# Second context attention: the first batch's keys projected in the norm's stage, and two sets of banks for the first unit's scan

## The reference, cut to what matters

```
q = (layernorm(x) @ Wq + bq)   k = (context @ Wk + bk)   v = (context @ Wv + bv)   (per head)
attn = clip(q k^T * 8**-0.5, -10000, 10000)
attn = softmax(attn)           (where any is nan: 1/1601)
x = x + (attn v) @ Wo + bo
```

## Time and profile before

| | |
|---|---|
| median of 3 runs | 4416.74 us (4416.56 to 4418.13) |
| profiled execution: span from the first to the last instruction | 4419.3 us, 2.6 above the median; no other time is recorded for it |
| busy: PE, DVE, ACT, POOL | 3412.6, 2996.2, 1886.4, 352.4 us |
| mean granted TensorE clock | 0.872 |
| this attention's stages, preparing stage to the end of the ticks | 1788.3 to about 2407 us |

### The profile page before, as it was taken

The page is one execution under the profiler, slowest core; times in us unless marked ns, Lnnn a source line. Parts: engine busy times, 40 slices in busy tenths (PEclk is TensorE's granted clock), DMA queues, the critical chain, the costliest instruction groups (busy, mean ns, idle before and its releaser), DMA issues. The chain is left out here.

```text
span 4419.3 us, 53028 instructions
## 1 busy us (share of the span) xinstructions
PE 3412.6 (77%) x21138; PEld 1815.2 (41%) x21138; DVE 2996.2 (68%) x4093; ACT 1886.4 (43%) x2165; POOL 352.4 (8%) x150
## 2 busy tenths in 40 slices
PE   5799999999999975577776786266654669577579
PEld 3434444444444433234333654222222346454357
DVE  4467776777677767388998545689998554546642
ACT  2255555555555543134443133344443134345233
POOL 0000000000000000100000000024443000000000
PEclk9799999999999987699999798566666798688789
DMA  2000000000000000100000300100000101010000
GB/s 79 9 0 0 0 1 0 0 0 0 0 1 0 0 6 7 25 14 9 9 1 3 117 2 2 46 0 0 0 0 0 39 2 39 9 39 1 1 31 14
DMA packets 13082, 56.19 MB, mean 13 GB/s; under 512 B 2209, under 2 KB 2721, under 8 KB 12066
## 3 DMA queue, kind: packets, MB, share of 16 engines
q1 hardware_dynamic: 12834, 52.78, 3.9%
HBM read 48.97 MB, written 0.52 MB: 11 GB/s over the span
## 5 line engine op out<-in xcount | busy, mean ns | idle before, releaser
L1019 PE MATMUL banks<-L0x_q_context,L0x_context 96*128 96x512 f32 x1600 | 725.7, 596 | 11.2 <-ACT L0x_ring L1086 9.9
L1030 PE MATMUL banks<-L0x_ring,L0x_context_rows 128*101 128x512 f32 x1600 | 721.3, 594 | 2.9 <-ACT L0x_ring L1076 2.9
L1086 ACT COPY L0x_ring<-banks 128x1024 f32<-128x1024 f32 (+1 forms) x416 | 404.3, 980 | 604.5 <-PE banks L1019 604.5
L1130 DVE TENSOR_TENSOR L0x_maxima<-L0x_maxima,L0x_ring 128x1024 f32<-128x1024 f32 (+1 forms) x288 | 332.7, 1165 | 228.3 <-ACT L0x_ring L1086 228.2
L1114 DVE TENSOR_TENSOR L0x_ring<-L0x_ring,L0x_greatest 128x2048 f32<-128x2048 f32 (+1 forms) x208 | 466.5, 2245 | 20.8 <-ACT L0x_ring L1086 19.3
L1019 PEld LDWEIGHTS banks<-L0x_q_context,L0x_context 96*128 96x128 f32 x1600 | 303.0, 191 | 396.9 <-issue 375.9
L1030 PEld LDWEIGHTS banks<-L0x_ring,L0x_context_rows 128*101 128x101 f32 x1600 | 267.8, 168 | 411.6 <-issue 406.4
L1076 ACT ACTIVATE L0x_ring<-L0x_ring 128x2048 f32<-128x2048 f32 (+1 forms) x208 | 384.2, 1848 | 11.1 <-DVE L0x_ring L1114 10.7
L1521 ACT ACTIVATE L1x_probs<-banks 128x2048 f32<-128x2048 f32 (+1 forms) x112 | 196.6, 1755 | 260.3 <-PE banks L1451 218.4
L1554 DVE TENSOR_REDUCE L1x_maxima<-banks 128x3 f32<-128x1203 f32 (+1 forms) x176 | 241.6, 1373 | 92.3 <-PE banks L1420 92.3
L1420 PE MATMUL banks<-L1x_k,L1x_q 32*128 32x401 f32 x1024 | 181.4, 591 | 120.4 <-DVE L1x_maxima L1554 105.1
(11 more groups left out here) (943 smaller groups left out, 5258.2 us busy)
## 6 DMA issues: line engine op xcount, KB each, us to landing
L1f_expert_weights<-in_L1f_experts SPq DMA_DIRECT2D x16, 512.0 KB, 10.3
L2f_expert_weights<-in_L2f_experts SPq DMA_DIRECT2D x8, 512.0 KB, 5.3
L3a_expert_weights<-in_L3a_experts SPq DMA_DIRECT2D x8, 512.0 KB, 6.0
L3f_expert_weights<-in_L3f_experts SPq DMA_DIRECT2D x8, 512.0 KB, 6.5
L1x_k<-L1x_k_rows SPq DMA_DIRECT2D x64, 50.0 KB
L0x_context<-in_context SPq DMA_DIRECT2D x1, 2401.5 KB, 19.6
L1x_context<-in_context SPq DMA_DIRECT2D x4, 600.4 KB, 5.2
L2x_contexts<-in_context SPq DMA_DIRECT2D x1, 2401.5 KB, 18.2
```

The costliest lines, as they stand in the source:

```text
L1019: mm = pe.matmul(k.ps[0:height(j), i, :], c1[:, j * P:j * P + height(j)], q1[:, u // 2 % 2, :], start=True, stop=True)
L1030: mm = pe.matmul(k.ps[0:CW, bank, :], rows1[0:height(j), j, :], ring[0:height(j), s % RING, i, :], start=s == FIRST[u] and i == 0, stop=s ...
L1086: act.copy(ring[0:r, s % RING, 2 * p:2 * p + len(pair), :], k.ps[0:r, 2 * p:2 * p + len(pair), :]).then_inc(copied, 1)
L1130: dve.tensor_tensor(o, before, ring[0:r, s % RING, 2 * p:2 * p + m, :], ALU.max).then_inc(maxed, 1)
```

## The change

For the first batch the key projection, its bias and the spreading DMAs leave `attend_clipped` and go to the stage of the norm, as an object `FirstKeys` that `normalise_columns` calls: first in PE's list, after the root in ACT's, alone in SP's. The first unit's scan uses banks 0 to 2 for even bursts and 3 to 5 for odd ones, and waits for the reduce of the burst before last. The slot of the first batch's values comes after the first unit's turn, and the first three slots alternate with the first three of the second unit's bursts.

```diff
@@ normalise_columns(..., keys=None)
+        if keys:
+            @block.sync
+            def _(sp):
+                keys.spread(sp)
         @block.tensor
         def _(pe):
+            if keys:
+                keys.project(pe)
             for t in range(tiles):
@@
             act.activation(k.sd[:, 0:tiles], k.ve[:, 0:tiles], ACT.Sqrt).then_inc(sd_ready, 1)
+            if keys:
+                keys.place(act)
@@
-X_SLOTS = [("keys", 0), ("values", 0), ("floor", 0), ("pair", 0)]
+X_SLOTS = [("values", 0), ("floor", 0), ("pair", 0)]
@@
+class FirstKeys:
+    def project(self, pe):
+        pe.wait_ge(self.arrived[0], 16)
+        for i, (c, m) in enumerate(CHUNKS):
+            mm = pe.matmul(self.k.ps[:, 3 + i, 0:m], self.w["k"], self.context[:, 0, c:c + m], start=True, stop=True)
+        mm.then_inc(self.projected, 1)
+    def place(self, act):
+        act.wait_ge(self.projected, 1)
+        act.activation(self.k_rows[:], self.k.ps[:, 3:7, :].rearrange("p a n -> p (a n)")[:, 0:CTX], ACT.Identity,
+                       bias=self.w["bk"]).then_inc(self.placed, 1)
+    def spread(self, sp):
+        d = 8
+        sp.wait_ge(self.placed, 1)
+        for h in range(16):
+            sp.dma_start(self.kT[32 * (h % 4):32 * (h % 4) + d, 0, h // 4, :], self.k_rows[d * h:d * h + d, :]).then_inc(self.here, 16)
@@ attend_clipped
+        def scan_bank(m):
+            return 3 if m < NB and m % 2 else 0
@@ SP
-            spread(0)
             load(2)
@@ scan(m)
-                if g == 0 and burst == 0:
-                    pe.wait_ge(spread_keys, 16 * H * (b + 1))
+                if u == 0 and burst == 0:
+                    pe.wait_ge(first_keys.here, 16 * H)
+                elif g == 0 and burst == 0:
+                    pe.wait_ge(spread_keys, 16 * H * b)
-                if m:
+                if u == 0 and m >= 2:
+                    pe.wait_ge(reduced, m - 1)
+                elif u:
                     pe.wait_ge(reduced, m)
@@ PE, ahead of the loop
-            for slot in X_SLOTS[0:2]:
-                fill(slot)
             for m in range(NB):
                 scan(m)
             turn(0)
-            for slot in X_SLOTS[2:FIRST_SLOTS]:
+            early = [m for n in range(SCAN_FROM, 0) for m in bursts_in(n)]
+            for i, slot in enumerate(X_SLOTS[0:FIRST_SLOTS]):
                 fill(slot)
-            for n in range(SCAN_FROM, 0):
-                for m in bursts_in(n):
-                    scan(m)
+                scan(early[i])
+            for m in early[FIRST_SLOTS:]:
+                scan(m)
```

More of the change, by code:

```diff
@@ L223, with normalise_columns @@
 ACT_TILES = (3, 6, 7)
-def normalise_columns(k, src, rows, dstT, gain=None, shift=None, column_gain=None, column_shift=None, eps=1e-5, values=None, tiles=TILES):
+def normalise_columns(k, src, rows, dstT, gain=None, shift=None, column_gain=None, column_shift=None, eps=1e-5, values=None, tiles=TILES, keys=None):
     shared = [t for t in ACT_TILES if t < tiles] if gain is None else ()
@@ L1365, with __init__, attend_clipped @@
 SLOT = {slot: n for n, slot in enumerate(X_SLOTS)}
-def attend_clipped(k, w, qT, context, c_sum, marks, limit, pick, y, arrived, bufs):
+class FirstKeys:
+    def __init__(self, k, ctx, w, context, arrived, k_rows, kT):
+        self.k, self.w, self.context, self.arrived, self.k_rows, self.kT = k, w, context, arrived, k_rows, kT
+        self.projected, self.placed, self.here = (ctx.enter_context(k.nc.semaphore("L1x_first_keys_" + n))
+                                                  for n in ("projected", "placed", "spread"))
+    def project(self, pe):
[12 more added lines that the diff above has]
+            sp.dma_start(self.kT[32 * (h % 4):32 * (h % 4) + d, 0, h // 4, :], self.k_rows[d * h:d * h + d, :]).then_inc(self.here, 16)
+def attend_clipped(k, w, qT, context, c_sum, marks, limit, pick, y, arrived, first_keys, bufs):
     d, H, G = 8, 16, 4
@@ L1411, in scan @@
                 b, g = X_UNITS[u]
-                if g == 0 and burst == 0:
-                    pe.wait_ge(spread_keys, 16 * H * (b + 1))
+                if u == 0 and burst == 0:
+                    pe.wait_ge(first_keys.here, 16 * H)
+                elif g == 0 and burst == 0:
+                    pe.wait_ge(spread_keys, 16 * H * b)
                 if burst == 0 and u:
                     pe.wait_ge(shifted, u)
-                if m:
+                if u == 0 and m >= 2:
+                    pe.wait_ge(reduced, m - 1)
+                elif u:
                     pe.wait_ge(reduced, m)
+                bank = scan_bank(m)
                 for i, item in enumerate(BURSTS[burst]):
                     it, c, h = ITEMS[item]
-                    mm = pe.matmul(k.ps[:, i, 0:WIDE], qT[row(h), g, b * S + it * P:b * S + (it + 1) * P],
+                    mm = pe.matmul(k.ps[:, bank + i, 0:WIDE], qT[row(h), g, b * S + it * P:b * S + (it + 1) * P],
                                    kT[row(h), b % 2, g, 400 * c:400 * c + WIDE], start=True, stop=True)
@@ L1501, in take @@
                 if kind == "keys":
-                    if at:
-                        act.wait_ge(spread_keys, 16 * H * at)
+                    act.wait_ge(first_keys.here, 16 * H)
+                    if at > 1:
+                        act.wait_ge(spread_keys, 16 * H * (at - 1))
                     act.activation(k_rows[:], k.ps[:, 3:7, :].rearrange("p a n -> p (a n)")[:, 0:CTX], ACT.Identity, bias=w["bk"]).then_inc(taken, 1)
@@ L1661, in _ @@
                 act.copy(kT[:, 0].rearrange("p g n -> p (g n)"), k.row31[:].broadcast_to([P, G * CTX]))
-        normalise_columns(k, k.x, k.z, k.zT)
+        first_keys = FirstKeys(k, ctx, w, context, arrived, bufs[0], kT)
+        normalise_columns(k, k.x, k.z, k.zT, keys=first_keys)
         linear_columns(k, [(qT[:, g, :], [(w["q"][:, g * P:(g + 1) * P], k.zT)], bq[:, g:g + 1], d ** -0.5, None) for g in range(G)])
-        attend_clipped(k, w, qT, context, c_sum, marks, limit, pick, y, arrived, bufs)
+        attend_clipped(k, w, qT, context, c_sum, marks, limit, pick, y, arrived, first_keys, bufs)
         with k.stage() as (block, signal):
```

2 lines of the change are left out of this document (1 added, 1 removed).

## The result

The changed kernel takes 4398.31 us (median of 4 runs, 4391.98 to 4398.65); four runs of the kernel before have a median of 4417.43. The medians differ by 19.1 us. The ratio of the runs is 0.9947, with a 95% interval of 0.9933 to 0.9961, so by the ratio 23.4 us are saved (17 to 30) where 30.8 were forecast. The median lies 12.3 us above the forecast and 1.3 above its range; by the ratio, the 4416.74 that the forecast started from become 4393.3, 7 us above the forecast and inside the range. The direction is right, and the gain came out a quarter smaller than forecast. A second set of five runs of the same kernel gave 4398.75 and 0.9946 (0.9934 to 0.9959).

A forecast was written before the change was run, and what follows sets the result against it. DVE was taken to bound the main loop; before it, SP's issues and PE and DVE alternating set the time. Gains 7.95 + 19.0 + 3.9 = 30.8 us take the median from 4416.74 to 4386 us, range 4380 to 4397.

The forecast's parts named there:

- SP's issues hold the stage: Norm's stage: it ends only after SP's 16 issues (10.81 us), so the query projection starts 11.2 us later.
- estimate of 8.6 us: Query projection: would start 8.6 us earlier if each SP issue took the skill page's 50 ns, not 0.68 us.
- First reduce: Start of the first unit's scan: first DVE reduce at 1825.35 instead of 1833.30, gain 7.95 us.
- The two sets of banks: First unit's scan: PE and DVE overlap, first reduce to gathering 14.4 us instead of 33.4, gain 19.0 (16.2 at low clock).
- I take full clock, nearer to the first: First unit's scan: PE, busy 0.71, keeps clock 1.00, as a 0.64 stretch did; one with 0.53 fell to 0.87.
- The lead: Gathering to the main loop's first clip: with the turn, gain 3.9 us (between -0.8 and 5.5).
- My own figure for a low clock throughout: Turn to first clip: at low clock throughout it takes 21.6 us, 0.8 worse than now.
- The loop costs nothing: Main loop: bound by DVE and unchanged at 515 us, so it adds nothing to the sum.
- the rival that made the kernel slower: Main loop: over 88 us more at low clock, at 0.35 us lost each, would eat the 30.8 us; chance 0.02.
- low clock through scan and lead: Rival for the first scan and stretch to first clip: 7.95 + 16.2 - 0.8 = 23.3 us gained, 4393; chance 0.16.

The follow-up runs named there:

- spread in the query stage: Changed kernel with SP's 16 key-spreading issues moved from the norm's stage to the query projection's stage; ratio 0.9931 to the kernel before.
- banks only: Changed kernel keeping only the two bank sets; keys projected and spread at the attention's head, order as before; ratio 0.9963 to the kernel before.
- busy scan: Changed kernel with unneeded matmuls of zeros filling PE's idle time in the first unit's scan and up to the main loop; ratio 0.9935 to the kernel before.
- held clock: As "all busy, late values", but the 256-column matmul of zeros in PE's wait for the keys' landing issued five times, not once; ratio 0.9929 to the kernel before.
- all busy, late values: Changed kernel, values still after the turn, with SP's issues in the query projection's stage and matmuls of zeros in PE's pauses; ratio 0.9947 to the kernel before.
- busy loop: Changed kernel with two of the four matmuls of each pair's fill in the main loop issued twice; ratio 1.0084 to the kernel before.

## Why the prediction was right or wrong

- **SP's issues hold the stage**: right. 19.14 for the start of the query projection against 18.6; PE's key projection took 5.78 (5.55), the meeting of the engines 0.89 after SP's last issue (0.6). The 16 issues took 10.81 us again, beside other work too (spread in the query stage). The dispatch figure of about 50 ns in the Trainium skill ("DMA: Bandwidth & Descriptors", "Anatomy of one DMA — SWDGE (gpsimd) path") stands there for DMAs that GpSimd issues. These were issued by SP, so the figure is not given for them, and the prediction's estimate of 8.6 us took it beyond what the page says; the 0.68 us of the row held.
- **First reduce**: right, 8.2 us gained against 7.95. POOL, busy 3.00 of 3.00 us in the window from 1824.4, did not slow the reduces beside it.
- **The two sets of banks**: the mechanism is right, at both clocks (1.62 a burst at low, banks only; 14.18 and 14.20 for the scan at full, busy scan and held clock). The gain was 17.4 instead of 19.0. The Trainium skill's kernel in which double-buffering PSUM gave no further gain ("TensorE: Matmul & The Clock Gate", "HAM oscillation") is no guide here: the second set of banks alone gave 16.3 us (banks only).
- **"I take full clock, nearer to the first"**: this is the step that failed. I compared PE's busy share, 0.71, with a stretch of the loop at 0.64 that kept 1.00. In the scan the clock fell nevertheless, in the window from 1827.4. The share of busy time alone does not tell the clock: in the run with late values PE was busy all the time at 0.50. The cost of this step is 15.97 us for the scan where 14.4 were forecast; at full clock it was 14.18 (busy scan).
- **The lead**: 0.7 us gained instead of 3.9, for the same reason. It was costed from a full clock at the turn; at the turn the clock was already low. My own figure for a low clock throughout, 0.8 worse than now, was nearer, 1.5 off. With the clock held ahead of it the lead was 17.71 (busy scan), against 18.1 forecast.
- **The loop costs nothing**: wrong by 3.2 us. Its work is unchanged, but its low stretches lie elsewhere: eleven distances between exponentials differ, by 0.2 to 3.2 us each, and make up all of it. The prediction had priced a us at the low level at 0.35 us from PE's average share of the loop, and only in the rival that made the kernel slower; in its sum the loop stood at nothing. It also called the loop bound by DVE; with room to spare it is so only in two of a unit's seven distances, and in the others the chain of PE and ACT has less than 0.7 us of room (busy loop).

The terms: 8.2 + 17.4 + 0.7 - 3.2 = 23.1, and 0.2 at the turning of the results, 23.3 in all. The rival "low clock through scan and lead" had 23.3 too. That its figure is met to the tenth is luck: its scan gained 16.2 and its lead lost 0.8, and its loop was free. In kind it is the rival that came nearest, for the clock was low in most of the scan and of the lead.

Open is why the low stretches of the loop fall where they do. The repeats show that it is not chance from one execution to the next, but which entry gives 517 and which 522 I cannot say; the same holds for the 2.8 us behind the attention. That filling PE's pauses can keep the clock high was shown ahead of the loop only; in the loop itself the one trial changed the critical chain as well.

## What to carry to other kernels

When work is moved to an earlier stage to hide its latency, ask of every queue in that stage, the DMA queue too, whether it outlasts the others: here 16 issues of 0.68 us made a stage of 10 us last 19, and moving them one stage further, beside 10 us of matmuls, took 7.2 us of waiting away. Cost a stretch behind a change at both levels of PE's clock, and do not infer the level from a busy share elsewhere. Cheap matmuls in PE's pauses can hold a high clock if they start while it is high. Started at the low level they were a gamble here: 7.5 us lost in one scan, the clock back soon in some leads and late in another. And compare a loop piece by piece, from one repeat of an instruction to the next, before calling it unchanged: two loops with the same work and nearly the same mean clock differed in eleven places.

## What the runs showed of the hardware that was not expected

- The granted clock fell from 1.00 to 0.50 in a scan where PE was busy in 0.95 of every 1.32 us, the pauses 0.37 us long (changed kernel, rows from 1825.99); with one more matmul of zeros in each pause it stayed at 1.00 for 14 us, and for some 12 us when that matmul used a quarter of PE's rows.
- At 0.50 it did not rise in the scan's 24.7 us with PE busy throughout (all busy, late values: matmuls on three row groups of 32 rows, and 128-row matmuls of zeros between), whereas under the query projection's matmuls of 512 columns, which start at 1811.59 in the changed kernel, it was 0.50 in the window from 1812 to 1815 and 0.98 in the next, from 1815 to 1818. Under one and the same list of matmuls behind the turn it was back about 3 us after its fall in the busy scan and some 17 us after it in the held clock. What makes the difference was not tried.
- The loop's clips repeated to 0.02 us over 490 us, low stretches and all, in two executions of the changed kernel, and to 0.03 us in another kernel that enters the loop in the same way (spread in the query stage), on another chip than the repeat.
